# Experts by pairs of tiles, a rewritten attention and routing stage, and one comparison of all tile columns at a time, in a gated cross-attention layer with a mixture of experts

## The reference

```
def attention(Q, K):                                 # V = K = ctx, lens = _lenS2
    scores = einsum('bqd,bkd->bqk', Q, K) / sqrt(256)
    mask = (qpos >= lens) & (kpos >= lens)
    attn = softmax(where(mask, -1e13, scores))
    return (attn @ K) @ W.T + b
def experts(x):                                      # x: 4096 rows
    routing = softmax(x @ router_w.T)
    top_w, top_i = top_k(routing, 2); top_w /= sum(top_w)
    y_e = (silu(x @ w_gate[e].T) * (x @ w_up[e].T)) @ w_down[e].T
    return sum over the two chosen e of top_w[e] * y_e
x = x + tanh(g_xattn) * attention(layernorm(x), ctx)
x = x + tanh(g_ffn) * experts(layernorm(x))
```

## Time and profile before

| | |
|---|---|
| median of 3 runs | 480.4 us |
| the profiled execution's own time | 478.07 us |
| its span | 476.2 us |
| TensorE busy | 422.5 us (89%) |
| VectorE busy | 239.4 us (50%) |
| ScalarE busy | 192.2 us (40%) |
| GpSimd busy | 242.1 us (51%) |
| granted TensorE clock, mean | 0.909 of 2.4 GHz |
| chain that ended last | PE 77%, DVE 11%, DMA 3%, ACT 3% |

### The profile page before, as it was taken

One profiled execution on the slowest core, in us unless ns is written; L12 is line 12 of the kernel. 1 busy time (PEld: TensorE's weight loads), 2 busy tenths in 40 slices (PEclk: granted clock), 3 DMA queues, 4 the chain that ended last, 5 costly groups with the idle time before them and its releaser, 6 DMA issues.

```text
span 476.2 us, 9017 instructions
## 1 busy us (share of the span) xinstructions
PE 422.5 (89%) x2491; PEld 356.2 (75%) x2492; DVE 239.4 (50%) x748; ACT 192.2 (40%) x480; POOL 242.1 (51%) x310
## 2 busy tenths in 40 slices
PE   7988886630669999999999999999999999999994
PEld 3847665420448888888888888888888898888884
DVE  3115899989935555555555543333333333333331
ACT  2353655302024555454545543343433333343331
POOL 8421676753053555265645555556554645555552
PEclk9595889555589999999999999999999999999999
DMA  6714566688521333833543334243333332423342
GB/s 196 234 46 133 192 214 219 211 284 274 210 70 22 49 67 49 305 55 57 105 124 60 56 56 66 47 67 51 62 55 57 48 63 45 67 45 56 56 66 27
DMA packets 31943, 49.59 MB, mean 104 GB/s; under 512 B 3516, under 2 KB 25489, under 8 KB 31921
## 3 DMA queue, kind: packets, MB, share of 16 engines
q0 software_dynamic: 13152, 18.65, 23.6%
q1 hardware_dynamic: 17511, 29.84, 18.6%
q10 hardware_dynamic: 1258, 0.84, 0.6%
HBM read 31.76 MB, written 17.57 MB: 104 GB/s over the span
## 4 chain that ended last, share of the span: by engine, by line
PE 77%; DVE 11%; DMA 3%; ACT 3%; issue 2%; POOL 2%; POOLq 0%; SPq 0%; ACTq 0%; DVEq 0%
PE GT L1088 19%; PE Y L1115 19%; PE UP L1088 19%; PE HT L1105 6%; PE S L997 4%; PE XT L1079 3%; PE O L1030 3%; DVE at_low L766 2%; DVE at_tile L877 2%; DMA out_rows<-y,idx 2%; ACT ex L559 1%; DVE xg L795 1%; DMA kr<-in_router 1%; DVE st L799 1%; PE O L1016 1%
## 5 line engine op out<-in xcount | busy, mean ns | idle before, releaser
L499 POOL DMA_INDIRECT out_rows<-y,idx x67 | 107.7, 1608 | 141.5 <-ACT y L625 90.2
L1115 PE MATMUL Y<-w_high,hT 128*128 x536 | 107.1, 283 | 0.0
L1088 PE MATMUL GT<-w_high,xtT 128*128 x272 | 102.7, 418 | 0.4 <-issue 0.4
L1088 PE MATMUL UP<-w_high,xtT 128*128 x272 | 102.0, 416 | 0.0
L930 DVE TENSOR_TENSOR hT<-HT,hT 128x512 fp32r<-128x512 f32 x67 | 46.4, 692 | 107.2 <-ACT hT L619 107.2
L491 POOL DMA_INDIRECT xt<-xn_rows,idx x71 | 70.9, 999 | 38.3 <-issue 20.7
L1115 PEld LDWEIGHTS Y<-w_high,hT 128*128 128x128 f32 x536 | 87.7, 190 | 3.0 <-issue 0.3
L625 ACT ACTIVATE y<-Y,xt 128x256 f32<-128x256 f32 x67 | 31.8, 474 | 139.8 <-PE Y L1115 114.3
L1115 PE MATMUL Y<-w_low,hT 128*128 x268 | 67.2, 283 | 0.0
L920 DVE TENSOR_TENSOR xtT<-XT,xtT 128x256 fp32r<-128x256 f32 x69 | 29.3, 425 | 59.6 <-ACT xtT L611 59.5
L1088 PEld LDWEIGHTS GT<-w_high,xtT 128*128 128x128 f32 x272 | 51.4, 189 | 10.3 <-issue 0.9
(11 more groups left out here) (158 smaller groups left out, 531.5 us busy)
## 6 DMA issues: line engine op xcount, KB each, us to landing
raw<-in_weights SPq DMA_DIRECT2D x16, 768.0 KB, 6.6
xn_rows<-pay SPq DMA_DIRECT2D x8, 528.0 KB, 3.2
xTg<-in_xT SPq DMA_DIRECT2D x8, 512.0 KB, 5.9
xg<-in_x SPq DMA_DIRECT2D x8, 512.0 KB, 5.1
out_rows<-xg SPq DMA_DIRECT2D x8, 512.0 KB, 3.3
xt<-xn_rows,idx POOLq DMA_INDIRECT x71, 2.8
out_rows<-y,idx POOLq DMA_INDIRECT x67, 3.8
kr<-in_ctx_rows SPq DMA_DIRECT2D x1, 308.0 KB
```

Of the source, the lines that this page charges most:

```text
L499: gp.indirect_dma_start(out=out, out_offset=bass.IndirectOffsetOnAxis(ap=idx[:, j:j + 1], axis=0), in_=y[:, j % 2, :], in_offset=None, com ...
L1088: last = mm(bank[:], xtT[:, s % 2, px, c * P:(c + 1) * P], parts[pw][c][:, bass.ds(e * HW + k * HID, HID)], start=(c == 0 and n == 0), sto ...
L1115: last = mm(Y[:, s % 2, 0:D], hT[:, px, c * P:(c + 1) * P], parts[pw][c // (HC // DC)][:, bass.ds(e * HW + DOWN + c % (HC // DC) * D, D)], ...
```

## The change

**Experts.** Places go by 256 (a pair of tiles), and each expert begins at a multiple of 256. The weights are now the stationary operand, 128 by 128, and the pair's 256 places move; hidden comes out transposed, so its transposes go. Hidden is worked in two halves q of 256 units. The high and low parts of a whole expert are no longer kept: raw holds all experts, and in every turn ACT and DVE cut the next pair's expert, gate and up in two halves (`cut_gate_up`, 1,024 elements a partition each) into gu, of which there is one for each half, and down (`cut_down`, 1,024) into dn, of which there are two. TensorE's turn is gate and up of half 1, four transposes of the pair two ahead, gate of the next pair's half 0, down (24 matmuls), up of the next pair's half 0. The pair has two gathers, two scalings and two adds, in order, each add still behind the landing of the one before. Loads of the experts 4 to 7 follow the first eight gathers, a quarter of an expert at a time.

**First stage.** The row sums of the attention's result come out of the product too (RW = 9 columns into bank M), so `sum_squares2` on ACT takes the place of the statistics on DVE. The scaling of exponentials on POOL goes: the reciprocals are applied as DVE adds the rows (`add_rows`), and the gate and the bias go into vw (`values`). Scores run up to four groups ahead; the values of batches 2 and 3 are formed in the loop; at_low is built in pieces between other steps; the masks move from POOL to DVE. `keep_busy` products of 512 columns stand at the start, in every turn of the loop and around the list.

**The list.** at_tile is compared 16 units at a time, with float16 operands, units innermost; the table of experts is made behind idx.

```diff
+RW = NE + 1
+OW = D + RW
 EPS = 1e-5
 MASKED = -float(2 ** 100)
 
-TILES = (TOPK * N - NE) // P + NE
-TW = TILES + 1
+PT = 2 * P
+PAIRS = (TOPK * N - NE) // PT + NE
+LEAST = TOPK * N // PT
+TILES = 2 * PAIRS
 UNITS = TOPK * NT
 CU = TOPK * G
+CHUNK = 2 * CU
 ROW = D + NE
 CW = D
-XR = 8
-AHEAD = 6
-TURNS = (TILES - 2) // XR
-HALF_CODE = N // 2
+XR = 4
+AHEAD = XR
 
...
 HALVES, HW = DC, DOWN + HC // DC * D
-CUTS = 4
-PIECE = HALVES * HW // CUTS
-EARLY, LATE = 3, 3
+PARTS = 4
+PW = HALVES * HW // PARTS
...
+        def each_pair(eng, turn):
+            with eng.Fori(0, LEAST // XR) as i:
+                carried = None
+                for s in range(XR):
+                    carried = turn(XR * i + s, s, i, carried)
+            used = eng.value_load(pairs_used[:], min_val=LEAST, max_val=PAIRS)
+
+            def rest(j, carried):
+                if j < PAIRS:
                     with eng.If(used > j):
-                        tile(j)
-                        rest(j + 1)
-
-            rest(TURNS * XR)
+                        rest(j + 1, turn(j, j % XR, j // XR, carried, PAIRS - 1 - j))
+
...
+            def load_weights(e, parts):
+
+                if 0 < e < 4 and parts[0] == 0:
+                    sp.wait_ge(raw_loaded, 16 * PARTS * e)
+                for part in parts:
+                    sp.dma_start(raw[:, e, part * PW:(part + 1) * PW],
+                                 weights[e].rearrange("p h n -> p (h n)")[:, part * PW:(part + 1) * PW]
+                                 ).then_inc(raw_loaded, 16)
 
...
                     load_x(k + 4)
-                if k >= GROUPS - EARLY:
-                    load_weights(k - (GROUPS - EARLY), raw_loaded if k == GROUPS - EARLY else raw_next)
+                if k + 6 < GROUPS:
+                    sp.wait_ge(scores_ready, k + 5)
+                    load_xT(k + 6)
+                if k >= GROUPS // 2:
+
+                    e, part = divmod(PARTS // 2 * (k - GROUPS // 2), PARTS)
+                    load_weights(e, range(part, part + PARTS // 2))
+            load_weights(2, range(PARTS))
             store_xn(GROUPS - 1)
-
-            sp.sem_inc(raw_late, RAW_LATE0)
-            load_weights(EARLY, raw_late)
...
+
+                sp.wait_ge(tile_loaded[s], 32)
+            for e in range(4, NE):
...
+            def add(j, t):
+
+                pool.wait_ge(y_added, 16 * (2 * j + t) + Y_ADDED0)
+                pool.wait_ge(y_ready, 2 * j + t + 1 + Y_READY0)
+                gp.indirect_dma_start(
+                    out=out, out_offset=bass.IndirectOffsetOnAxis(ap=idx[:, 2 * j + t:2 * j + t + 1], axis=0),
+                    in_=y[:, j % 2, t, :], in_offset=None, compute_op=ALU.add).then_inc(y_added, 16)
+
...
+            def sum_squares2(k):
+                act.wait_ge(negmean2_ready, k + 1)
+                for t in range(G):
+                    act.wait_ge(rows_added, k * G + t + 1)
+                    last = nc.scalar.activation(squares2[:, t], rows(k, t), ACT.Square, bias=negmean2[:, k % 2, t:t + 1],
+                                                accum_out=ssq[:, k % 2, G + t:G + t + 1])
+                last.then_inc(ssq2_ready, 1)
 
...
+            def cut_gate_up(j, e, q):
+
+                act.wait_ge(up_ready, 2 * j + q - 1)
+                nc.scalar.copy(gu[:, 0, q], gate_up_of(e, q)).then_inc(gu_high[q], 1)
+
...
+                act.wait_ge(down_ready, 2 * j - 2 + DOWN0)
+                nc.scalar.copy(dn[:, 0, b], down_of(e)).then_inc(dn_high, 1)
+
+            def tile_highs(j, b):
...
+            def turn(j, s, i, known=None, behind=2):
+
+                e, e1 = known or (weights_of(j), weights_of(j + 1) if behind > 0 else None)
+                e2 = None
+                if behind > 0:
+                    act.wait_ge(raw_loaded, 16 * PARTS * (e1 + 1))
+                    cut_gate_up(j + 1, e1, 0)
+                hid_highs(j, 0)
+                silu(j, 1)
+                if behind > 1:
+                    tile_highs(j + 2, s % 2)
+                hid_highs(j, 1)
+                if behind > 0:
+                    silu(j + 1, 0)
+                    cut_gate_up(j + 1, e1, 1)
+                    cut_down(j + 1, e1, (s + 1) % 2)
+                if behind > 1 and s < XR - 1:
+                    e2 = weights_of(j + 2)
                 weigh(j, s, e)
-
-            with act.Fori(0, NE // 2 - 1) as i:
-
-                act.wait_ge(raw_late, 16 * HALVES * 2 * i + RAW_LATE0)
-                act.sem_inc(passed_act)
...
+            def values(b):
+
+                dve.wait_ge(vw_ready, b + 1)
+                stt(out=vw[:, b], in0=W[0:CTX, 0:OW], scalar=gates[0:CTX, 0:1], in1=bias[:],
+                    op0=ALU.mult, op1=ALU.add).then_inc(vw_copied, 1)
 
...
-                    after(added[t // 2])
-                    last = v.bn_stats(st2[:, t], rows(k, t))
...
+                def add_rows(t):
+                    return stt(out=rows(k, t), in0=O[:, t // 2, t % 2 * D:(t % 2 + 1) * D], scalar=rg[:, q, t:t + 1],
+                               in1=rows(k, t), op0=ALU.mult, op1=ALU.add)
+
+                scaled = mark(tt(out=lg0[:], in0=M[:, 0:G * RW].rearrange("p (t e) -> p t e", t=G),
+                                 in1=rg[:, q].unsqueeze(2).to_broadcast([P, G, RW]), op=ALU.mult))
+                add_rows(0).then_inc(rows_added, 1)
+                after(scaled)
+                summed = mark(tt(out=lg1[:], in0=lg0[:], in1=sr[:, q], op=ALU.add))
+                add_rows(1).then_inc(rows_added, 1)
+                after(summed)
+                ts(negmean2[:, q], lg1[:, :, NE], -1.0 / D, None, ALU.mult).then_inc(negmean2_ready, 1)
+                add_rows(2).then_inc(rows_added, 1)
+                add_rows(3).then_inc(rows_added, 1)
+                behind = k - 2
+                at_lows(behind, range(0, 2))
+                if k == 0:
...
-                for t in range(G):
-                    last = v.bn_aggr(mv[:, t], st2[:, t])
-                moments = mark(last)
+                    router_part(n)
+                if k > 0:
+                    own = own_ranks(k - 1)
+                    at_lows(behind, range(2, 3))
+                    ranked = unit_ranks(k - 1, own)
+                    at_lows(behind, range(3, 4))
+                    masked = low_bits(k - 1, ranked)
+                    at_lows(behind, range(4, 5))
+                    low_places(k - 1, masked)
+                dve.wait_ge(ssq2_ready, k + 1)
                 if more:
-                    first_variances(n)
...
+            counted = mark(v.tensor_copy(ntf[:], nts[:]))
+            at_lows(last_group, range(2, 3))
+            after(counted)
+            counted = mark(v.tensor_tensor_scan(cum[:], one8[:], ntf[:], 0.0, ALU.mult, ALU.add))
+            at_lows(last_group, range(3, 4))
...
+            after(begun)
+            dve.wait_ge(tile_iota, 1)
+            for c in range(UNITS // CHUNK):
+                tt(out=at_tile[:, c], in0=iota_t[:],
+                   in1=col[:, c * CHUNK:(c + 1) * CHUNK].unsqueeze(1).to_broadcast([P, TILES, CHUNK]),
+                   op=ALU.is_equal).then_inc(tile_hot, 1)
 
...
+            def cut_gate_up(j, e, q):
+                dve.wait_ge(gu_high[q], j + 1)
+                low_of(gu[:, 1, q], gate_up_of(e, q), gu[:, 0, q]).then_inc(gu_low[q], 1)
+
...
+            def turn(j, s, i, e=None, behind=2):
+                gate_up(j, 0)
+                if behind > 0:
+                    e1 = weights_of(j + 1)
+                    cut_gate_up(j + 1, e1, 0)
+                hid_lows(j, 0)
+                gate_up(j, 1)
+                if behind > 1:
+                    tile_lows(j + 2, s % 2)
+                hid_lows(j, 1)
+                if behind > 0:
+                    cut_gate_up(j + 1, e1, 1)
+                    cut_down(j + 1, e1, (s + 1) % 2)
...
+            keep_busy(4)
+            scores(1)
...
-                    last = mm(O[:, t, 0:OW], eT[:, t * P:(t + 1) * P], vw[:, b, :], start=True, stop=True)
+                    keys = eT[:, t * P:(t + 1) * P]
+                    mm(M[:, t * RW:(t + 1) * RW], keys, vw[:, b, D:OW], start=True, stop=True)
+                    last = mm(O[:, t // 2, t % 2 * D:(t % 2 + 1) * D], keys, vw[:, b, 0:D], start=True, stop=True)
                 last.then_inc(attn_ready, 1)
...
                 if k > 0:
                     ranks(k - 1)
-                if k + 3 < GROUPS:
-                    scores(k + 3)
+                if k + 1 < GROUPS:
+                    pe.wait_ge(rows_added, (k + 1) * G)
+                    attention(k + 1)
+                if k < 2:
+                    pe.wait_ge(vw_copied, k + 2)
+                    keep_busy(10 if k == 0 else 5)
+                    values(k + 2)
+                elif k + 1 < GROUPS:
+                    pe.wait_ge(vw_copied, BATCH)
+                    keep_busy(5)
                 if k + 2 < GROUPS:
                     transpose_exp(k + 2)
-
-            pe.wait_ge(carry_ready, GROUPS)
```

(56 more changed lines are left out.)

## The result

The changed kernel takes 439.73 us (median of 4 runs, 437.68 to 441.32) where the kernel before, run beside it, takes 479.6 us (476.0 to 485.05): a ratio of 0.917, 95% interval 0.909 to 0.925. The profiled execution took 437.68 us, a span of 435.9.

The account below looks back on a forecast made before the run. TensorE bounds the expert tiles before the change, POOL's adds after it. 28 + 54 + 21 us to the list, 21.5 to the first add, 315 of adds and 5.2 give 444.7; with 1.8 around, 446 us, range 429 to 464.

Parts of the forecast that it names:

- first added rows: First stage, start to the first group's added rows: between 24 and 33 us, taken as 28.
- seven turns: Group loop: 7.7 us a turn where it was 8.93, 54 us for seven; ends 7.3 and 8.9.
- last rows to the list: Last group's added rows to the finished list of places: 21.1 us, where it was 28.3.
- the cuts cost nothing: Expert pairs: splitting weights again in every pair adds nothing on TensorE; 2.4 us needed in a 3.3 us window.
- so the adds become the bound: POOL's queue: two adds a pair need at least 9.2 us against TensorE's 9.14; taken as 4.7 us an add.
- rival A: Expert pairs: the adds keep up and TensorE bounds; 436 us, class 427 to 438, chance 0.24.
- the forecast's own class: Whole kernel: measured times of 438 to 455 us, given chance 0.50.
- Rival D: First stage stays at half clock, unread products lengthen it by 10 to 12 us: 457 us; chance 0.19 together with C.
- C: Pairs: VectorE waits for POOL's issues or ACT lacks room; turn 9.7 to 10.1, some 455 to 470; 0.19 with Rival D.
- E: POOL's queue: each add's issue waits a whole cut, over 5.3 us an add; 493 us, slower; chance 0.03.
- Rival B: List: half-precision comparisons run at twice the float32 row's rate, 2.8 us less, 443 us; chance by itself 0.6.
- Rival F: List: units-innermost layout makes the products' moving operand strided, 2 to 4 us if twice the cost, 449; inside the forecast's 0.50.

Follow-up runs that it names:

- experiment 6: Changed kernel with VectorE taking the low part of the first half of gate and up twice in each pair: 476.78 us, ratio 0.992.
- experiment 1: Changed kernel with the two waits ahead of an add in the earlier kernel's order, row values first, then landing: 465.22 us, ratio 0.974.
- experiment 3: Changed kernel with one of three partial products of gate and up left out, for less TensorE work: 427.31 us, ratio 0.890.
- experiment 4: Changed kernel with the add of the second 128 rows of each pair left out: 436.74 us.
- experiment 8: Changed kernel without the ten unread products of the first turn, those of later turns kept: 439.22 us.
- experiment 7: Changed kernel without the unread products inside the eight turns of the first stage: 442.67 us, ratio 0.924.
- experiment 9: Changed kernel with places innermost in the one-hot columns, still in half precision: 439.06 us.
- experiment 10: Changed kernel with four units innermost in the one-hot columns instead of sixteen: 438.53 us.

## Why the prediction was nearly right, and where it was wrong

The change saves 40 us against the forecast's 32, counted from the profiled 478.07 to 446. Term by term, in us:

```
                               predicted   measured
first added rows                   28.0       22.3
seven turns                        54.0       58.0
last rows to the list              21.0       24.5
list to first add                  21.5       20.3
first add to last                 315.0      305.2
last add to the end                 5.2        5.6
span                              444.7      435.9
```

**Pairs on TensorE.** 34 pairs, 0.121 us a matmul, 9.14 us a pair: measured 34, 0.120, 9.12. That the cuts cost nothing held, or nearly: the spare room of 0.9 us (3.3 against 2.4) was a quarter of that (experiment 6). In three pairs of four the low half is ready 2.55 us behind the end of up, and TensorE goes on to it at 3.07. In every fourth, the first pair of a round of the loop, it is ready at 3.0 (298.9 to 301.9) and used at 3.3, since ScalarE begins its cast 0.6 us late; these are the pairs of 9.3 us.

**The step that failed: "so the adds become the bound", at 4.7 us each.** What happened is rival A. I took the floor of 4.6 us from the earlier trace rows as if it belonged to the transfer. 0.5 us of it belonged to the place of the landing's wait in the instruction stream, and the diff moves that wait: it writes the wait for the landing first. (Nor was 4.6 the floor of the old order: other adds of the kernel before are 4.38 us apart.) With the old order the adds are the bound and 4.96 us apart, just above my 4.6 to 4.93 (experiment 1); with the new one their floor is 4.38 (experiment 3), under TensorE's 4.56. The sign of being wrong that the prediction named, adds closer than 4.55 us, is there: 4.35 and 4.10. That the median still fell between 438 and 455, the forecast's own class, is luck: the mechanism is A's, whose sum gave 436 us with the list at 103 us, where it came at 104.8, and the profiled execution of 437.68 lies in A's class. The meeting with cuts was priced fairly: issues of 1.85 us for 1.59 are there in one add of three, and up to 2.6 us in experiment 3, but with TensorE as the bound they cost nothing (experiment 4). So what I read of the Trainium skill, "SBUF — State Buffer", section "Who interferes with whom", agrees with these rows, and speaks against this change only where the adds bound it. The 23 adds and 25 gathers of the changed kernel (from 135 us on) that start while a VectorE operation on two SBUF operands is under way, over 0.2 us of it left, are longer by 0.25 and 0.87 us on average, with 0.37 and 0.98 us of it left; the 64 that start with none under way and during which one begins are not (0.02 us at most). So an issue waits for the rest of the operation, which is why the 0.24 us of the earlier trace rows is less than a whole one.

**Start of the first stage.** 22.3 us lies below my lower end of 24. The keys land at 6.9 us where I took 8.0 from the kernel before. Scores cost 1.97 us each, at the full clock, the key transposes under 0.5 us for my 1.3, and attention 2.7 us for 2.0; of the wait of 1 to 2 us, 0.3 is left. The parts of the rewritten first stage were not run one by one, so what each gives stays open.

**Turns.** Six of them take 7.84 us on average against 7.7. The seventh, the first, takes 10.98: two scores groups, 2.2 us each, and ten unread products, 2.16 us together. Without these it takes 9.53 (experiment 8). I gave all turns one price; the diff shows the first to be another.

**Rival D** did not happen because the unread products hold the clock: taken out, it falls to the half (experiment 7). My 10 to 12 us were for half the clock with the products in place, which no run shows; half the clock without them costs 3 us. **Rivals C and E** did not happen either: VectorE's cuts of gate and up last 1.22 us throughout (1.227 at most), in whatever way they meet POOL's issues, and the longest issue of an add is 1.87 us.

**List.** From the last added rows to the comparisons 13.2 us, as summed (13.3). Rival B was right: 0.72 us a comparison where the float32 row gives 1.42. This is the rate that the Trainium skill gives for it, in "VectorE: DVE Perf Modes", section "The perf-mode tier table (the rule you actually need)"; that estimate of 2.9 us was met by 2.96. Rival F was right in kind and mis-sized: I added 2 to 4 us to products of which only the last 16 stood on the path, but with comparisons of 0.72 us all 64 do, 9.31 us for the 1.1 in my sum. B and F came as one: the layout that gives the comparisons their rate moved the path from VectorE to TensorE (experiments 9 and 10). Together they made the list 3.4 us later than forecast.

The profiled span is 8.8 us shorter than forecast mostly by the adds (10 us), with the first rows (6 us) against turns and list (4 and 3 us); the median of 439.73 lies 2 us above the profiled execution.

## What to carry to other kernels

When a floor is read from a row, read also which wait was slow there and how it stands in the instruction stream: of two waits ahead of an indirect transfer, write first the one that will end last and often. A layout that speeds the producer has to be priced at the consumer too, each element's distance included. And where stages hand over, a step made earlier is only worth what the next late thing (here the landing of the first gathers, then the clock) lets through.

## What the runs showed of the hardware that was not expected

A wait that rides on the indirect transfer lets it start 0.3 us behind the landing (experiment 3); a wait as an instruction of its own 0.8 to 0.9 us (experiment 1 and the kernel before).

A float16 moving operand of 78 columns read 32 bytes apart costs 0.143 us a matmul and 8 bytes apart 0.072 (experiment 10). Both are the same before and behind 96 us, where the granted clock falls from 1.00 to 0.50, so the distance sets them and not the clock. Contiguous columns cost 0.04 us at the full clock and 0.065 at the half (experiment 9). Half-precision comparisons keep the double rate with an innermost run of four elements (experiment 10).

POOL's issues grow where a VectorE operation on two SBUF operands had begun before them, by about what is left of it: adds from 1.59 to 1.85 us and gathers from 0.99 to 1.9 in the changed kernel, and adds up to 2.6 us in experiment 3. One that begins during the issue does not lengthen it.
